# Causal attention on one core: softmax denominators from a column of ones, division with tokens on partitions, one output matmul, per-token norm

## The reference, cut to what matters

```
x = jax.random.normal(ks[0], (B, T, D_MODEL))          # a sequence: 256 tokens x 128 features
W_qkv = uniform((D_MODEL, 3 * D_MODEL)), b_qkv = uniform((3 * D_MODEL,))
W_proj = uniform((D_MODEL, D_MODEL)),    b_proj = uniform((D_MODEL,))

def _softmax(x, axis=-1): return jax.nn.softmax(x, axis=axis)

def _layernorm(x, axis=-1, eps=1e-05):
    m = jnp.mean(x, axis=axis, keepdims=True)
    v = jnp.var(x, axis=axis, keepdims=True)
    return (x - m) / jnp.sqrt(v + eps)
```

## Time and profile before

| | us |
|---|---|
| median of 3 runs | 4724.15 (4722.18 to 4735.0) |
| the profiled execution | 4729.9 |
| its span in the trace | 4728.0 |
| of it, slots 2 to 15 of the attention stage | 569.9 |
| of it, the drain of the stage (slots 16 to 18) | 62.8 |

### The profile page before, as it was taken

The page is one execution under the profiler, slowest core; times in us unless marked ns, Lnnn a source line. Parts: engine busy times, 40 slices in busy tenths (PEclk is TensorE's granted clock), DMA queues, the critical chain, the costliest instruction groups (busy, mean ns, idle before and its releaser), DMA issues. The chain is left out here.

```text
span 4728.0 us, 193017 instructions
## 1 busy us (share of the span) xinstructions
PE 4220.1 (89%) x74452; PEld 3406.3 (72%) x74465; DVE 3795.1 (80%) x6502; ACT 3363.7 (71%) x5951; POOL 2753.7 (58%) x3197
## 2 busy tenths in 40 slices
PE   7889976697366899999999999999999999999997
PEld 4444433376254788878887888888887888888886
DVE  5777755644336899989999999989999999999995
ACT  4555521255134789979988899888998889888995
POOL 3222213634324677767776777767776777677772
PEclk8989878799677999999999999999999999999998
DMA  3000004252221211121111111121112111121111
GB/s 154 1 0 0 0 0 121 90 189 84 88 76 45 54 44 42 49 59 50 43 45 55 52 49 43 43 67 43 48 43 61 48 46 45 44 66 44 49 42 38
DMA packets 141887, 255.23 MB, mean 54 GB/s; under 512 B 34160, under 2 KB 56944, under 8 KB 137072
## 3 DMA queue, kind: packets, MB, share of 16 engines
q1 hardware_dynamic: 133520, 235.49, 17.0%
q0 software_dynamic: 8192, 17.84, 1.2%
HBM read 70.76 MB, written 44.04 MB: 24 GB/s over the span
## 5 line engine op out<-in xcount | busy, mean ns | idle before, releaser
L2566 POOL TENSOR_TENSOR d_rc<-d_rc,d_rs 128x512 f32<-128x512 f32 x768 | 964.0, 1277 | 463.0 <-DVE d_rs L2649 447.6
L2576 POOL TENSOR_TENSOR d_rc<-d_rc,d_inv 128x1024 f32<-128x1024 f32 x384 | 722.9, 1903 | 128.2 <-DVE d_inv L2670 127.9
L2132 PE MATMUL d_pair<-d_W_high,d_xs_high 128*128 128x512 f32 x1152 | 519.1, 451 | 117.4 <-issue 34.4
L2649 DVE TENSOR_TENSOR d_rc<-d_pair,d_rot 128x512 f32<-128x512 f32 x768 | 527.5, 687 | 93.7 <-ACT d_sq L2381 75.7
L2381 ACT ACTIVATE d_sq<-d_pair 128x512 f32<-128x512 f32 x768 | 435.2, 596 | 138.9 <-PE d_pair L2132 133.8
L2649 DVE TENSOR_TENSOR d_rs<-d_pair,d_rot 128x512 f32<-128x512 f32 x768 | 522.1, 680 | 0.0
L2132 PE MATMUL d_pair<-d_W_high,d_xs_low 128*128 128x512 f32 x1152 | 461.4, 401 | 0.0
L2132 PE MATMUL d_pair<-d_W_low,d_xs_high 128*128 128x512 f32 x1152 | 460.7, 400 | 0.4 <-issue 0.4
L2659 DVE TENSOR_REDUCE d_ss<-d_sq 128x16 f32<-128x1024 f32 x384 | 448.2, 1208 | 0.0
L2279 PE MATMUL d_pair<-d_OT,d_Wo 128*128 128x128 f32 x3072 | 380.7, 278 | 0.0
L2176 PE MATMUL d_pair<-d_ident,d_rc 128*128 128x128 f32 x3072 | 367.5, 273 | 1.0 <-ACT d_sq L2381 1.0
(11 more groups left out here) (378 smaller groups left out, 11104.5 us busy)
## 6 DMA issues: line engine op xcount, KB each, us to landing
d_VW<-d_V SPq DMA_DIRECT2D x768, 128.0 KB
d_VW<-d_V SPq DMA_DIRECT2D x576, 64.0 KB
leaf_rows<-a_zeros SPq DMA_DIRECT2D x12, 1152.0 KB, 14.6
q_xrow<-leaf_rows SPq DMA_DIRECT2D x24, 576.0 KB
leaf_out<-q_yrow SPq DMA_DIRECT2D x24, 512.0 KB
d_W_whole<-Wqkv_dram SPq DMA_DIRECT2D x7, 1536.0 KB, 6.4
f_xrow<-leaf_rows SPq DMA_DIRECT2D x8, 576.0 KB, 3.6
b_table<-q_w_dram SPq DMA_DIRECT2D x4, 1024.0 KB, 8.0
```

The lines of the kernel that those rows point to most:

```text
L2132: mm = nc.tensor.matmul(target, x_part[:, t.par, :], w_part[:, c, :], start=n == 0, stop=n == 2)
L2566: nc.gpsimd.tensor_tensor(own[:, :, a, :], own[:, :, a, :], other[:, :, 1 - a, :], ALU.add).then_inc(s[f"add{qk}_ready"], 1)
L2576: nc.gpsimd.tensor_tensor(heads(rc[:, t.par, half, :]), heads(rc[:, t.par, half, :]), inv[:, t.par, half, :].unsqueeze(2).to_broadcast([12 ...
L2649: ins = nc.vector.tensor_tensor(heads(target), heads(ps[:, j, :]), rot[:, t.par, half, cs, :].unsqueeze(1).to_broadcast([128, HP, DH]), AL ...
```

## The change

The weights V get a ninth column of ones for each head (of the 32 that are there), so that the matmul with the values gives the denominators too; the four quarters with the ones matrix go. ScalarE copies the raw result of each two groups out of PSUM (`take_values`), TensorE turns it so that tokens are on partitions (`values_turned`, four transposes each), VectorE takes the reciprocal of 16 denominators for each token and multiplies 128x128 (`normalised`), TensorE turns the result back (`turned_back`, two transposes), ScalarE copies it (`take_turned_back`), and one output matmul with an unpadded W_proj is left. The variance becomes one number for each token (two matmuls with one column), the root and the reciprocal run on 128x2, and `spread` (two matmuls) brings the result back onto all partitions for `layernorm`. W_proj is 64 KB where it was 256 KB.

```
-        V_AFTER = {0: (0,), 2: (1,), 4: (2, 3), 8: (4,), 10: (5, 6), 11: (7,)}
+        V_AFTER = {0: 0, 2: 1, 4: 2, 6: 3}
...
+            def attend(t, par, G):
...
+                if G == 2:
+                    wait(pe, "x_ready", t - 1)
+                bank, at = banks[6 + G // 2], 256 * (G % 2)
...
+            def values_turned(t, gp):
...
+                wait(pe, "raw_ready", t, 2, gp + 1)
+                for tile in range(2):
+                    for g in range(2):
+                        at = 256 * tile + 128 * g
+                        mm = nc.tensor.transpose(banks[6 + gp][:, at:at + 128], raw[:, gp, 256 * g + 128 * tile:256 * g + 128 * tile + 128],
+                                                 ident[:])
...
+            def turned_back(t):
...
+                wait(pe, "y_ready", t, 2)
+                for tile in range(2):
+                    mm = nc.tensor.transpose(banks[6][:, 128 * tile:128 * tile + 128], y[:, tile].rearrange("p h d -> p (h d)"), ident[:])
...
-                wait(pe, "y_ready", t, 2)
-                for g in range(A_G):
-                    mm = nc.tensor.matmul(banks[6][:, 0:T], Wp[:, g, :], Y[:, g, :], start=g == 0, stop=g == A_G - 1)
-                mm.then_inc(s["out_done"], 1)
+                wait(pe, "yt_ready", t)
+                nc.tensor.matmul(banks[7][:, 0:T], Wp[:], yT[:], start=True, stop=True).then_inc(s["out_done"], 1)
...
-                nc.tensor.matmul(banks[6][:, 0:T], mean_w[:], xsq[:], start=True, stop=True).then_inc(s["var_done"], 1)
+                for half in range(2):
+                    mm = nc.tensor.matmul(banks[6][:, half:half + 1], xsq[:, 128 * half:128 * half + 128], mean_w[:, 0:1], start=True, stop=True)
+                mm.then_inc(s["var_done"], 1)
...
+            def spread(t):
...
+                wait(pe, "rstd_ready", t)
+                for half in range(2):
+                    mm = nc.tensor.matmul(banks[7][:, 128 * half:128 * half + 128], rstd[:, half:half + 1].to_broadcast([128, 128]), ident[:],
+                                          start=True, stop=True)
...
-                nc.vector.reciprocal(rsum[:], banks[7][:]).then_inc(s["rsum_ready"], 1)
-                wait(dve, "rsum_ready", p, 2, gp + 1)
-                nc.vector.tensor_tensor(Y[:, 2 * gp:2 * gp + 2, :].rearrange("p g t -> p (g t)"), banks[6][:], rsum[:], ALU.mult)\
...
+                turned = banks[6 + gp][:].rearrange("p (t h c) -> p t h c", t=2, c=32)
+                nc.vector.reciprocal(rden[:, gp], turned[:, :, :, A_DH]).then_inc(s["rden_ready"], 1)
+                wait(dve, "rden_ready", t, 2, gp + 1)
+                nc.vector.tensor_tensor(y[:, :, 8 * gp:8 * gp + 8, :], turned[:, :, :, 0:A_DH],
+                                        rden[:, gp].unsqueeze(3).to_broadcast([128, 2, 8, A_DH]), ALU.mult).then_inc(s["y_ready"], 1)
```

More of the change, by code:

```diff
@@ L72, in causal_attention @@
         mean_w = sb("mean_w", [128, 128])
-        ones = sb("ones", [128, 32])
         eps = sb("eps", [128, 1])
@@ L86, in causal_attention @@
         PTb = sb("PTb", [128, 2, 4, A_G, 128])
-        rsum = sb("rsum", [128, 512])
-        Y = sb("Y", [128, A_G, T])
+        raw = sb("raw", [128, 2, 512])
+        rden = sb("rden", [128, 2, 2, 8])
+        y = sb("y", [128, 2, A_HEADS, A_DH])
+        yT = sb("yT", [128, T])
         r = sb("r", [128, T])
@@ L91, in causal_attention @@
         xsq = sb("xsq", [128, T])
[L92 to L93 removed]
+        std = sb("std", [128, 2])
+        rstd = sb("rstd", [128, 2])
         zeros = sb("zeros", [128, 16 * ROW])
@@ L289, in slot @@
                         project(k, par, QK_AFTER[job])
-                    for quarter in V_AFTER.get(job, ()):
-                        attend(t, par, quarter)
+                    if job in V_AFTER:
+                        attend(t, par, V_AFTER[job])
+                    if job == 1:
+                        spread(u)
+                    if job == 5:
+                        values_turned(t, 0)
+                    if job == 9:
+                        values_turned(t, 1)
                 values(k, par)
@@ L294, in slot @@
                     scores(k, par, job)
-                    if job == 6:
+                    if job == 1:
+                        turned_back(t)
+                    if job == 4:
                         output(t)
-                    if job == 9:
+                    if job == 8:
                         mean(t)
@@ L340, in exponentials, with take_values, take_turned_back @@
                                      scale=float(A_DH) ** -0.5).then_inc(s["pt_ready"], 1)
+            def take_values(t, gp):
+                if not live(t):
+                    return
+                wait(act, "pv_done", t, 4, 2 * gp + 2)
+                wait(act, "turned_done", t - 1, 2, gp + 1)
+                nc.scalar.activation(raw[:, gp, :], banks[6 + gp][:], ACT.Copy).then_inc(s["raw_ready"], 1)
+            def take_turned_back(t):
+                if not live(t):
+                    return
+                wait(act, "back_done", t)
+                wait(act, "out_done", t - 1)
+                nc.scalar.activation(yT[:], banks[6][:, 0:T], ACT.Copy).then_inc(s["yt_ready"], 1)
             def deviation(t):
@@ L360, in slot @@
                         first_piece(k, QK_AFTER[job])
+                    if job == 3:
+                        take_values(t, 0)
+                    if job == 7:
+                        take_values(t, 1)
                 second_piece(k, 6)
                 second_piece(k, 7)
+                take_turned_back(t)
             run(act, slot)
@@ L508, in centred, with inverse @@
                 nc.vector.tensor_tensor(xc[:], r[:], banks[7][:, 0:T], ALU.subtract).then_inc(s["xc_ready"], 1)
+            def inverse(t):
+                if not live(t):
+                    return
+                wait(dve, "std_ready", t)
+                wait(dve, "spread_done", t - 1)
+                nc.vector.reciprocal(rstd[:], std[:]).then_inc(s["rstd_ready"], 1)
             def layernorm(t):
@@ L512, in layernorm @@
                     return
-                wait(dve, "std_ready", t)
-                nc.vector.reciprocal(rstd[:], std[:]).then_inc(s["rstd_ready"], 1)
-                wait(dve, "rstd_ready", t)
-                nc.vector.tensor_tensor(X[:, t, PAD:], xc[:], rstd[:], ALU.mult).then_inc(s["x_ready"], 1)
+                wait(dve, "spread_done", t)
+                nc.vector.tensor_tensor(X[:, t, PAD:], xc[:], banks[7][:, 0:T], ALU.mult).then_inc(s["x_ready"], 1)
                 wait(dve, "x_ready", t)
@@ L535, in slot @@
                     row_maxima(k, job)
-                    if job == 2:
-                        normalised(t, 1)
-                    if job == 8:
+                    if job == 6:
                         residual(t)
```

70 lines of the change are left out of this document (33 added, 37 removed).

## The result

The changed kernel takes 4603.77 us (median of four runs, 4595.21 to 4607.38) against 4724.05 for the kernel before on the same chip: a ratio of 0.974, 95% interval 0.9725 to 0.9754, or 120.3 us less. The forecast was 4610, a gain of 114.

A forecast was written before the change was run, and what follows sets the result against it. TensorE's fixed order (work, waits, clock) was taken as the bound. 105 us saved over 14 slots plus 22 in the drain, less 13 for clock falls, gives 114, so 4724.15 becomes 4610 us; range 4588 to 4662.

The forecast's parts named there:

- The bound: Attention slots 2 to 15: TensorE's fixed order sets the pace through its work, waits and clock, at 40.71 us each.
- the wait for Y: TensorE's idle before the output matmuls, while VectorE's 128x512 reciprocal runs: 2.2 us a slot, expected to go.
- the wait before quarter 4: TensorE's idle ahead of the value matmuls' quarter 4: 0.65 us a slot, expected to go.
- the low clock: TensorE at 1.2 GHz for 7.3 us a slot; the part beyond the output expected to give back 1.8 us.
- What comes: Work added to TensorE per slot: ten transposes 1.2 us, spreading 0.55, variance nothing; 1.75 us in all.
- What is late next: New TensorE waits per slot: 0.7 us before score job 4, 0.2 before job 0, 0.6 for ScalarE's copies; 1.5 in all.
- The 0.6 for ScalarE's copies: First half of a slot: two more 128x512 copies on nearly full ScalarE, between 0 and 1.2 us, taken as 0.6.
- The falls: Clock drops in a slot's second half, behind waits before score jobs: 3 of 14 slots, 4.4 us each, 13 us.
- The drain: Slots 16 to 18, 62.80 us before: 29.6 off, 7.6 on, net 22 us less, range 15 to 25.
- Rival 1: Clock falls in nearly each slot, behind the wait for GpSimd's third pieces: slot 37.6, time 4661 us; chance 0.22.
- Rival 2: The norm's longer chain or ScalarE's copies hold TensorE 2 us more per slot: time 4638 us; chance 0.14.
- Rival 3: Slower than before: TensorE stays at 1.2 GHz through whole slots, slot 51 us, time 4844 us; chance 0.02.

The follow-up runs named there:

- b1_recip: Kernel before, with the two 128x512 reciprocals per sequence made on 16 columns only, most of the division left out; ratio 0.9793, slots 2 to 15 491.3 us.
- a1_ones: Changed kernel with every quarter of the value matmuls issued twice, into the same bank; ratio 0.9806, slots 2 to 15 503.3 us.
- a6_rawdve: Changed kernel with the two raw 128x512 copies per sequence on VectorE instead of ScalarE; ratio 0.9735, slots 2 to 15 465.1 us.
- a7_oldnorm: Changed kernel with the old norm: variance in one 128x256 matmul, root and reciprocal on 128x256, no spreading; ratio 0.9722, slots 2 to 15 460.1 us.
- a8_late_tr: a5_out6 with four more 32-bit 128x128 transposes between score jobs 3 and 4, from slot 0 on; ratio 0.9721, slots 2 to 15 468.0 us.
- a5_out6: Changed kernel with output and mean behind score jobs 6 and 9, residual behind the eighth maximum; ratio 0.9794, slots 2 to 15 492.1 us.
- a9_late_mm: a5_out6 with two plain 32-bit 128x128 matmuls between score jobs 3 and 4, from slot 0 on; ratio 0.9728, slots 2 to 15 467.9 us.
- a3_fill_tr: Changed kernel with four more 32-bit transposes of the identity between score jobs 3 and 4; ratio 0.9713, slots 2 to 15 459.7 us.

## Why the prediction was right, step by step

**The bound.** Right. Of the terms that go, the wait for Y, the wait before quarter 4, the low clock and the slow output all hang on the reciprocal, and b1_recip gave them back together: 78.7 / 14 = 5.6 a slot. The predicted terms that it covers are 2.2 + 0.65 + 1.8 and the output's fall from 638 to 392 ns (3.67 - 2.0 = 1.7), 6.3. By the two windows views, TensorE's idle time shrank by 2.6 a slot (58.7 us to 22.8) where the waits were put at 2.85, and its busy time by 3.1 (511.20 to 468.41) where the clock was put at 3.5. A part of the first is a wait of the mean for `a_r` (L271 above), which grew from 5.3 us in 14 slots to 7.4. The ones were put at 2.9 and are 2.4 to 2.6 by a1_ones.

**What comes.** Right. From start to start in slot 5, four raw transposes take 0.44, the pair of y 0.28, so ten take 1.16 (predicted 1.2); the spreading takes 0.45 (0.55); the variance 0.42.

**What is late next.** The total was near and its parts were not. The wait before job 4 was put at 0.7 from the 3.59 us between score jobs 0 and 4 of slot 1; it is 0.65, with 3.61 between the two jobs. The 0.6 for ScalarE's copies was added to it, and this is the mis-sized term: the second copy does hold the pieces up, by 0.49 (a6_rawdve), but that lies inside the 0.65 and TensorE waits for nothing else of ScalarE's. Before job 0 it waits for nothing (0.2). Quarter 2's wait for X was put at nothing, from slot 11 of before; it is 2.8 / 14 = 0.2, almost all of it in every second slot, together with another 0.34 before the first turned score job of that slot. So about 1.0 of waits came in place of 1.5, and less went than predicted (above), which cancels most of it. The slot without a fall is 33.0 on average, predicted 33.2.

**The falls.** Three were predicted and three came, twice, and in different slots. That the number was hit is partly luck: a1_ones with the same wait had two and a7_oldnorm none. What was argued, a fall behind the wait for the third piece and none behind the 0.75 to 0.83 before L272, is what every profile of the changed kernel and its variants shows. The price was too low: 4.4 predicted. Without a fall the slots sum to 32.0 + 7 x 32.6 + 6 x 33.3 = 460.0, so (475.5 - 460.0) / 3 = 5.2. The missing part is the two projections at the end of the slot, 3.57 in place of 1.99, which the prediction took for the place where the fall ends; half of their 1.6 comes back, since the 0.75 to 0.83 of idle before L272 is not there behind a fall (the row at 452.51 has none). The evidence that transposes hold the clock was thinner than the prediction has it: in the stretch of the earlier trace rows they are 32 of 199 matmul records. It was a8_late_tr that settled it, for short waits. Where the prediction says that the rule of the Trainium skill makes the second rival likelier, the first is meant, as it says itself further down.

**The drain.** Predicted 22, measured 21.9. The terms behind it can't all be told apart by these runs, but b1_recip's drain of 40.4 says that the reciprocals alone are worth 22.4, so part of the agreement is luck. Its granted clock is 0.92 there, where before has 0.66, so it also gets back the low clock that the prediction booked under output and ones. What is left of these two (13.6 off with the clock) must then cancel against raw copies, transposes and spreading (7.6 on); this is worked out and not shown. a7_oldnorm's drain is 2 to 4 us shorter, where the prediction has the new norm at 1.6 off and 0.8 on.

**The start.** W_proj's load was put at half a microsecond at most. Slot 1 starts 1.7 us earlier in the first pair of profiles and slot 2 2.0; over all profiles slot 1 starts between 45.2 and 49.8 us, so this is within its spread.

**The sum.** 94.4 + 21.9 + 2.0 is the 118.2 of the stage, but for rounding, against 92 + 22 + 0 = 114 predicted, and 120.3 by the medians.

**The rivals.** Rival 1, a fall in nearly each slot, is not the changed kernel, yet a5_out6 shows how near it was: output two jobs later, six falls. Rival 2, 2 us more a slot, fell by the changed kernel's own slots of 33.0: quarter 2 waits 0.2 for the norm, and ScalarE's copy is within the 0.65 before job 4. Rival 3 was never near: 0.96 mean clock.

What stays open: why the same 0.67 us wait is followed by a fall in some slots only. Counting kernels, with one profiled execution of each and two of the changed one, the ones with 9.0 us or more of idle before the score jobs had 3, 3, 2, 6 and 0 falls in 14 slots; the one with 4.7 had none; the six with 1.1 or less had none in 84 slots, nor did b1_recip. That work put into this wait removes the falls is shown (a8_late_tr, a9_late_mm); what decides between the slots is not.

## What to carry to other kernels

Look at what a slow VectorE instruction does to the engine that waits for it, not only at its own time: here 3.35 us of reciprocal cost 2.2 us of TensorE idle and then several more at 1.2 GHz. When one wait goes, find the next gap in TensorE's row and put work that is due anyway into it, 32-bit matmuls or transposes, before adding anything new. Where a change has several parts, price each alone: shortening the reciprocals alone gave over four fifths (78.7 of 94.4 us) of this one's gain in the slots, and the norm's part gave nothing. Work that is removed may have covered a wait: the ones behind the last projection did, as the rows of b1_recip and a1_ones read, and with them gone three falls took 15.5 us back.

## What the runs showed of the hardware

- In slots 2 to 15 of the changed kernel the granted clock fell from 1.00 to 0.50 behind an idle of 0.53 to 0.67 us among bf16 score jobs with 48 rows, in 6 of 28 slots, and stayed there for 13.7 us five times and for 20.5 us, into the drain, once. It did not fall behind 0.75 to 0.83 us of idle before L272, where two 32-bit projections (eight records) had run just before.
- Four 32-bit transposes of 128x128 (0.66 us) in that gap kept the clock at 1.00, as two 32-bit matmuls did (a8_late_tr, a9_late_mm: no fall in slots 1 to 15, where a5_out6 has seven).
- A reciprocal of 128x16 takes 248 ns, one of 128x512 3347; a copy of 128x512 on the same engine takes 0.68 us (a6_rawdve, L521).
- The later stages, the same code in every kernel here, take 4207 to 4218 us on two chips and 4001 to 4018 elsewhere, while slots of the attention stage agree to 0.1 us across chips: 32.6 and 33.3 in the changed kernel and in a3_fill_tr, 33.2 and 33.9 in a5_out6 and in a8_late_tr.
